# Rotary step of the second attention of layer two: neighbouring half blocks, cosine products in PSUM

## The reference, cut to what matters

```python
# hidden_states: (2, 512, 512); qkv_w: (512, 1536); H = 32 heads, D = 16
def _rope(x, cos, sin):
    x1, x2 = jnp.split(x, 2, axis=-1)
    return jnp.concatenate([x1 * cos - x2 * sin, x2 * cos + x1 * sin], axis=-1)
# q, k, v = (normalised x) @ qkv_w + qkv_b, 32 heads each; q, k = _rope(q), _rope(k)
# causal softmax(q k^T * scale) v, then out_w, out_b and the residual
```

## Time and profile before

| | |
|---|---|
| time, median of 3 runs | 2277.07 us (2275.81 to 2278.4) |
| profiled execution: its time, its span | 2275.74 us, 2273.9 us |
| mean granted TensorE clock | 0.953 |
| busy share of the span: PE, DVE, ACT, POOL | 92%, 62%, 51%, 36% |
| attn1b's first projection matmul starts | 1901.31 us |
| its first score matmul starts | 1999.34 us |

### The profile page before, as it was taken

The page is one execution under the profiler, slowest core; times in us unless marked ns, Lnnn a source line. Parts: engine busy times, 40 slices in busy tenths (PEclk is TensorE's granted clock), DMA queues, the critical chain, the costliest instruction groups (busy, mean ns, idle before and its releaser), DMA issues. The chain is left out here.

```text
span 2273.9 us, 33298 instructions
## 1 busy us (share of the span) xinstructions
PE 2086.4 (92%) x11568; PEld 1485.0 (65%) x11568; DVE 1400.9 (62%) x2517; ACT 1164.6 (51%) x2691; POOL 824.2 (36%) x996
## 2 busy tenths in 40 slices
PE   5999987999999999999987789999999887899988
PEld 3333345777888888888765667777777574654457
DVE  5788564536666666666646456666665565567756
ACT  4677543245656656656535455555555433235553
POOL 0000100235645645545520254555445213247611
PEclk9899978999999999999999799999999987989999
DMA  3000022671112112111011433443333003543301
GB/s 116 1 1 1 5 76 74 193 232 38 46 39 66 46 39 66 44 41 47 20 38 49 123 93 91 112 109 91 99 95 96 34 19 94 163 70 76 73 24 38
DMA packets 95427, 157.77 MB, mean 69 GB/s; under 512 B 11727, under 2 KB 33359, under 8 KB 93086
## 3 DMA queue, kind: packets, MB, share of 16 engines
q1 hardware_dynamic: 85662, 134.26, 20.6%
q0 software_dynamic: 9600, 21.38, 3.9%
HBM read 90.58 MB, written 31.46 MB: 54 GB/s over the span
## 5 line engine op out<-in xcount | busy, mean ns | idle before, releaser
L2528 POOL TENSOR_TENSOR attn1a_probs<-attn1a_probs,attn1a_recip 128x128 f32<-128x128 f32 (+3 forms) x256 | 178.9, 720 | 234.6 <-DVE attn1a_recip L2711 234.0
L1889 POOL TENSOR_TENSOR attn0b_probs<-attn0b_probs,attn0b_recip 128x128 f32<-128x128 f32 (+3 forms) x256 | 196.1, 787 | 184.9 <-DVE attn0b_recip L2133 184.9
L2584 ACT ACTIVATE attn1a_probs<-attn1a_scores,attn1a_negmax 128x128 f32<-128x128 f32 (+3 forms) x256 | 132.7, 523 | 175.4 <-DVE attn1a_negmax L2697 174.1
L1993 ACT ACTIVATE attn0b_probs<-attn0b_scores,attn0b_negmax 128x128 f32<-128x128 f32 (+3 forms) x256 | 132.7, 524 | 122.3 <-DVE attn0b_negmax L2126 121.7
L1440 DVE TENSOR_REDUCE attn0a_negmax<-attn0a_by_query 128x2 f32<-128x1024 f32 x128 | 151.9, 1219 | 11.8 <-PE attn0a_by_query L1557 11.8
L2697 DVE TENSOR_REDUCE attn1a_negmax<-attn1a_scores 128x2 f32<-128x256 f32 (+3 forms) x128 | 105.4, 823 | 71.4 <-PE attn1a_scores L2886 71.3
L1882 POOL TENSOR_TENSOR attn0b_q_cos<-attn0b_q_cos,attn0b_q_swap 128x512 f32<-128x512 f32 x64 | 84.3, 1317 | 159.9 <-DVE attn0b_q_swap L2115 159.9
L2001 ACT ACTIVATE attn0b_probsT_hi<-attn0b_turned 128x256 fp32r<-128x256 f32 (+3 forms) x128 | 90.1, 704 | 88.2 <-PE attn0b_turned L2277 86.6
L2126 DVE TENSOR_REDUCE attn0b_negmax<-attn0b_scores 128x2 f32<-128x256 f32 (+3 forms) x128 | 105.0, 820 | 46.7 <-PE attn0b_scores L2266 46.7
L2898 PE MATMUL attn1a_turned<-ident_f,attn1a_probs 128*128 128x128 f32 x640 | 116.1, 279 | 8.6 <-DVE attn1a_probsT L2705 7.3
L2112 DVE TENSOR_TENSOR attn0b_q_cos<-attn0b_aux,attn0b_cos_q 128x512 f32<-128x512 f32 x60 | 41.5, 691 | 116.2 <-ACT attn0b_q_swap L2014 116.2
(11 more groups left out here) (509 smaller groups left out, 6249.5 us busy)
## 6 DMA issues: line engine op xcount, KB each, us to landing
pre<-in_b_o SPq DMA_DIRECT2D x16, 1024.0 KB, 5.4
attn1a_qT<-attn1a_stage SPq DMA_DIRECT2D x128, 128.0 KB, 2.4
attn1a_qT<-attn1a_stage SPq DMA_DIRECT2D x64, 256.0 KB, 3.8
attn0b_vals<-attn0b_v_out SPq DMA_DIRECT2D x16, 512.0 KB, 3.9
attn0b_keys<-attn0b_part SPq DMA_DIRECT2D x32, 256.0 KB, 4.2
pre<-in_b_q SPq DMA_DIRECT2D x8, 1024.0 KB, 7.6
attn0b_kT<-attn0b_keys SPq DMA_DIRECT2D x64, 128.0 KB
pre<-in_b_kv SPq DMA_DIRECT2D x5, 1024.0 KB, 6.8
```

The lines of the kernel that those rows point to most:

```text
L1889: pool.tensor_tensor(x, x, recip[:, r % DEEP, e:e + 1].broadcast_to([P, (qt + 1) * P]), ALU.mult).then_inc(s_scaled, 1)
L1993: act.activation(probs[:, r % DEEP, e, 0:width], scores[r % 2][:, e, 0:width], ACT.Exp, bias=negmax[:, r % 2, e:e + 1], accum_out=sums[:, ...
L2528: pool.tensor_tensor(x, x, recip[:, r % DEEP, e:e + 1].broadcast_to([P, (qt + 1) * P]), ALU.mult).then_inc(s_scaled, 1)
L2584: act.activation(probs[:, r % DEEP, e, 0:width], scores[r % 2][:, e, 0:width], ACT.Exp, bias=negmax[:, r % 2, e:e + 1], accum_out=sums[:, ...
```

## The change

The columns of the key and query weights are reordered on the host so that a block holds one half (x1 or x2) of 16 heads, and its neighbour, the next block in the order, the other half of the same heads. The permutation matmul and its DMA go. ACT still writes raw (now four deep). DVE makes (projection + bias) x cosine straight from the projection's bank into one of four PSUM banks that the stage otherwise leaves idle (`turned`: by_key x 2, aux, out); POOL multiplies raw by the sines; DVE adds or subtracts the neighbour's sine product in the PSUM bank. PE now waits for the cosine product of block i - 2 instead of its raw. Splitting into hi and lo runs two blocks behind. The four pieces of a weight third are split one at a time (after blocks 1, 2, 4, 6 for the second third; 9, 10, 11, 12 for the last), and the last third's remainders are made by POOL. SP issues the last third's load behind the stores of part 6 instead of part 1, and the output weights' load behind everything, once the first attention tiles are in. A store now covers 16 heads x 8 rows instead of 8 heads x 16 rows.

```diff
-    blocks = [(kind, mt, b) for kind in range(KINDS) for mt in range(KT) for b in range(BATCH)]
+    RAWS = 4
+    SPLIT_SECOND, SPLIT_THIRD, SPLIT_THIRD_LO = (1, 2, 4, 6), (9, 10, 11, 12), (9, 11, 13, 14)
+    blocks = [(kind, 2 * half_heads + part, b) for kind in range(KINDS) for half_heads in range(2)
+              for b in range(BATCH) for part in range(2)]
...
-            raw, by_cos = take_sb("raw", [P, 2, SEQ]), take_sb("by_cos", [P, 2, SEQ])
-            turned_sb = take_sb("turned", [P, 2, SEQ])
...
+        turned = [by_key[0][:, :], by_key[1][:, :], aux_flat, out[:, :, :].rearrange("p t q -> p (t q)")]
+
+        def turned_block(k):
+            return k ^ 1
...
-            sp.dma_start(swap[:, :], d["c1_swap"]).then_inc(s_load, 16)
...
             def spread_out(i):
-                kind, mt, b = blocks[i]
-                into = spread_raw[kind][8 * mt:8 * mt + 8, :, bass.ts(b, SEQ)]
+                kind, mt, b = blocks[turned_block(i)]
+                heads, part = divmod(mt, 2)
+                into = spread_raw[kind][16 * heads:16 * heads + 16, :, bass.ts(b, SEQ)]
+                at = HD // 2 * part
                 sp.wait_ge(s_hi, i + 1)
-                sp.dma_start(into[:, 0:HD, :], part_hi[:, i % 2, :].bitcast(F32)).then_inc(s_spread[i % 2], 16)
+                sp.dma_start(into[:, at:at + HD // 2, :], part_hi[:, i % 2, :].bitcast(F32)).then_inc(s_spread[i % 2], 16)
                 sp.wait_ge(s_lo, i + 1)
-                sp.dma_start(into[:, HD:2 * HD, :], part_lo[:, i % 2, :].bitcast(F32)).then_inc(s_spread[i % 2], 16)
+                sp.dma_start(into[:, HD + at:HD + at + HD // 2, :], part_lo[:, i % 2, :].bitcast(F32)).then_inc(
+                    s_spread[i % 2], 16)
 
             load_weights(1)
             sp.dma_start(out_bias[:, :], d["c1_bo"].partition_broadcast(P)).then_inc(s_out_bias, 16)
             for i in range(NB):
                 spread_out(i)
-                if i == 1:
+                if i == SPLIT_SECOND[-1]:
                     load_weights(2)
-                if i == BLOCKS_OF_KIND + 1:
-                    sp.wait_ge(s_whi, 3 * KT)
-                    sp.wait_ge(s_wlo, 3 * KT)
-                    m.prefetch(sp, 0, w_in, d["c1_wo"].rearrange("(k p) o -> p k o", p=P))
+            for loaded in (s_kload[0], s_qload[0]):
+                sp.wait_ge(loaded, LOADED)
+            sp.wait_ge(s_whi, 3 * KT)
+            sp.wait_ge(s_wlo_v, KT)
+            m.prefetch(sp, 0, w_in, d["c1_wo"].rearrange("(k p) o -> p k o", p=P))
...
-            def times_cos(i):
-                kind, mt, b = blocks[i]
-                pool.wait_ge(s_raw, i + 1)
-                if i >= 2:
-                    pool.wait_ge(s_turned, i - 1)
-                pool.tensor_tensor(by_cos[:, i % 2, :], raw[:, i % 2, :], rope[:, kind, 0, :],
-                                   ALU.mult).then_inc(s_cos, 1)
+            def times_sin(k):
+                pool.wait_ge(s_raw, k + 1)
+                if k >= 2:
+                    pool.wait_ge(s_turned, k - 1)
+                pool.tensor_tensor(by_sin[:, k % 2, :], raw[:, k % RAWS, :], rope[:, blocks[k][0], 1, :],
+                                   ALU.mult).then_inc(s_sin, 1)
+
+            def split_value_weights(k):
+                pool.wait_ge(s_whi, KT * 2 + k + 1)
+                pool.tensor_tensor(w_lo[:, 0, k, :], w_in[:, k, :], w_hi[:, 0, k, :].bitcast(F32),
+                                   ALU.subtract).then_inc(s_wlo_v, 1)
...
-                times_cos(i)
+                times_sin(i)
+                if i in SPLIT_THIRD_LO:
+                    split_value_weights(SPLIT_THIRD_LO.index(i))
...
             def take(i):
                 kind, mt, b = blocks[i]
                 act.wait_ge(s_proj, i + 1)
-                if i >= 2:
-                    act.wait_ge(s_cos, i - 1)
-                    act.wait_ge(s_swap, i - 1)
-                act.activation(raw[:, i % 2, :], proj[i % 2], ACT.Identity,
+                if i >= RAWS:
+                    act.wait_ge(s_sin, i - RAWS + 1)
+                act.activation(raw[:, i % RAWS, :], proj[i % 2], ACT.Identity,
                                bias=bias_col[:, kind * KT + mt:kind * KT + mt + 1]).then_inc(s_raw, 1)
 
-            def split(i):
-                act.wait_ge(s_turned, i + 1)
-                if i >= 2:
-                    act.wait_ge(s_spread[i % 2], 16 * 2 * (i // 2))
-                act.activation(part_hi[:, i % 2, :], turned_sb[:, i % 2, :], ACT.Copy).then_inc(s_hi, 1)
+            def split(k):
+                act.wait_ge(s_turned, k + 1)
+                if k >= 2:
+                    act.wait_ge(s_spread[k % 2], 16 * 2 * (k // 2))
+                act.activation(part_hi[:, k % 2, :], turned[turned_block(k) % 4], ACT.Copy).then_inc(s_hi, 1)
...
+            for i in range(NB + 2):
                 if i < NB:
                     take(i)
-                if i == 1:
-                    split_weights(1)
-                if i >= 1:
-                    split(i - 1)
-                if i == BLOCKS_OF_KIND:
-                    split_weights(2)
+                if i >= 2:
+                    split(i - 2)
+                if i in SPLIT_SECOND:
+                    weights_hi(1, SPLIT_SECOND.index(i))
+                elif i in SPLIT_THIRD:
+                    weights_hi(2, SPLIT_THIRD.index(i))
...
-            def turn(i):
+            def weights_lo(third, k):
+                dve.wait_ge(s_whi, KT * third + k + 1)
+                dve.tensor_tensor(w_lo[:, third, k, :], w_in[:, k, :], w_hi[:, third, k, :].bitcast(F32),
+                                  ALU.subtract).then_inc(s_wlo, 1)
+
+            def times_cos(i):
                 kind, mt, b = blocks[i]
-                dve.wait_ge(s_swap, i + 1)
-                if i >= 2:
-                    dve.wait_ge(s_hi, i - 1)
-                dve.tensor_tensor(turned_sb[:, i % 2, :], by_key[i % 2][:, :], rope[:, kind, 1, :],
-                                  ALU.mult).then_inc(s_sin, 1)
-                dve.wait_ge(s_sin, i + 1)
+                dve.wait_ge(s_raw, i + 1)
+                if i >= 4:
+                    dve.wait_ge(s_lo, turned_block(i - 4) + 1)
+                dve.scalar_tensor_tensor(turned[i % 4], proj[i % 2], bias_col[:, kind * KT + mt:kind * KT + mt + 1],
+                                         rope[:, kind, 0, :], ALU.add, ALU.mult).then_inc(s_cos, 1)
+
+            def turn(k):
+                i = turned_block(k)
                 dve.wait_ge(s_cos, i + 1)
-                dve.tensor_tensor(turned_sb[:, i % 2, :], turned_sb[:, i % 2, :], by_cos[:, i % 2, :],
-                                  ALU.add).then_inc(s_turned, 1)
-
-            def split(i):
-                dve.wait_ge(s_hi, i + 1)
-                if i >= 2:
-                    dve.wait_ge(s_spread[i % 2], 16 * 2 * (i // 2))
-                dve.tensor_tensor(part_lo[:, i % 2, :], turned_sb[:, i % 2, :], part_hi[:, i % 2, :].bitcast(F32),
+                dve.wait_ge(s_sin, k + 1)
+                dve.tensor_tensor(turned[i % 4], turned[i % 4], by_sin[:, k % 2, :],
+                                  (ALU.subtract, ALU.add)[i % 2]).then_inc(s_turned, 1)
+
+            def split(k):
+                dve.wait_ge(s_hi, k + 1)
+                if k >= 2:
+                    dve.wait_ge(s_spread[k % 2], 16 * 2 * (k // 2))
+                dve.tensor_tensor(part_lo[:, k % 2, :], turned[turned_block(k) % 4], part_hi[:, k % 2, :].bitcast(F32),
                                   ALU.subtract).then_inc(s_lo, 1)
...
+            dve.wait_ge(s_load, 16)
+            for i in range(NB + 2):
+                if i < NB:
+                    times_cos(i)
+                    if i % 2 == 1:
+                        turn(i - 1)
+                        turn(i)
+                if i >= 2:
+                    split(i - 2)
+                if i in SPLIT_SECOND:
+                    weights_lo(1, SPLIT_SECOND.index(i))
...
-                    pe.wait_ge(s_raw, i - 1)
+                    pe.wait_ge(s_cos, i - 1)
...
-            def swap_halves(i):
-                pe.wait_ge(s_raw, i + 1)
-                if i >= 2:
-                    pe.wait_ge(s_sin, i - 1)
-                pe.matmul(by_key[i % 2][:, :], swap[:, :], raw[:, i % 2, :], start=True, stop=True).then_inc(s_swap, 1)
...
-                    pe.wait_ge(s_raw, NB - 1 + t)
+                    pe.wait_ge(s_cos, NB - 1 + t)
...
-                        pe.wait_ge(s_wlo, KT * 2 + k + 1)
+                        pe.wait_ge(s_wlo_v, k + 1)
...
-            for i in range(NB + 1):
-                if i < NB:
-                    project(i)
-                if i == 1:
-                    pe.wait_ge(s_load, 32)
-                if i >= 1:
-                    swap_halves(i - 1)
+            for i in range(NB):
+                project(i)
...
+    by_half = lambda x: t(x.reshape(-1, 2, 16, 2, 8), (0, 1, 3, 2, 4)).reshape(-1, DIM)
+    qkv = a["L1_attn_b_qkv_w"].reshape(DIM, 3, DIM)
```

(42 more changed lines are left out.)

14 lines of the change are left out of this document (6 added, 8 removed).

## The result

The changed kernel takes 2264.34 us (median of 6 runs, 2260.69 to 2269.03); the kernel before took 2277.74 us beside it (6 runs, 2275.81 to 2282.03). The ratio is 0.9941, with a 95% interval from 0.9927 to 0.9955: faster, by 13 us or so. The profiled execution took 2262.22 us.

A forecast was written before the change was run, and what follows sets the result against it. PE's own list was taken as the bound. The stage's terms summed to an end at 1987.1, 12.2 us earlier than 1999.3; from 2275.74 this made 2263.5, with 1.3 for the median 2264.8 us, range 2258.5 to 2272.5.

The forecast's parts named there:

- hole before block 12: PE waits for the last third of the weights, then its w_hi, raw and product: a hole of 2.6 us.
- wait before the values: Between block 15 and the value tiles: 0.7 us for the last product and POOL's last w_lo piece.
- hole before tile 2: Tile 0's value add queues on DVE behind the last three remainders: a 2.4 us hole, 1.5 for the clock behind it.
- Nothing gained up to block 4: Start of the stage: block 4 still starts near 1919.0; two saved swaps become idle time, 4.3 us in place of 1.84.
- Stores at 3.0 us: Part stores, DRAM side now led by 16 heads, not 8, land in 3.0 us instead of 5.05.
- Rival B: Stores still take 5.05 us to land: 6.5 us longer, 2271.3 us; chance 0.12.
- DVE writing PSUM: DVE's operations on PSUM take 0.68 us with a PSUM operand and 0.75 for the fused cosine product.
- rival C: DVE operations into PSUM take 1.05 us: the stage ends 5.7 us later, 2270.5 us; chance 0.08.
- rival A: Holes of 2.5 us do not bring PE's half clock: 3.5 us come back, 2261.3 us; chance 0.17.
- The third's load: SP's load of the last third of the weights, issued at 1938.1 behind part 6's stores, lands 5.9 us later.
- POOL's loads: Loads for the first attention steps: 18.6 us against 27.8 for the values, 9 us of cover; landing 3.4 us.
- Rivals D and E: D: more half-clock blocks on PE, 2277 us, chance 0.07. E: stores become the bound, 2285 us, slower, chance 0.06.

The follow-up runs named there:

- e3: The changed kernel with POOL's zeroing and copies spread over the gaps between its multiplications, its loads behind them: 2259.70 us, ratio 0.9934, stage 80.6 us.
- e1: The changed kernel with rows reordered so that each store's DRAM side is led by 8 again: 2271.89 us, ratio 0.9994, stage 91.9 us.
- e2: The kernel before, swaps kept, with rows reordered so that each store's DRAM side is led by 16: 2268.99 us, ratio 0.9977, stage 91.2 us.
- e4: The changed kernel with the second third split at blocks 1, 2, 3, 4, so the last third's load is issued earlier: 2261.88 us, ratio 0.9943.
- e7: The changed kernel with four spare matmuls (0.94 us) per block, putting the swaps' PE time back: 2268.37 us, ratio 0.9967, stage 90.5 us.
- e9: The changed kernel with the second third split earlier and spare matmuls before block 4's and value tile 2's waits: 2257.25 us, ratio 0.9919.

## Why the prediction was right, step by step

Terms of the stage, forecast and measured (from PE's timeline, whose main rows stand above; a block ends with its last matmul):

| term | forecast us | measured us |
|---|---|---|
| start to block 4 | 17.7 | 17.7 (hole 4.42, forecast 4.3) |
| block 4 at half clock | 4.9 | 4.6 |
| blocks 5 to 11 | 19.6 | 19.6 |
| hole before block 12 | 2.6 | 2.8 |
| blocks 12 to 15 | 13.2 | 13.0 |
| wait before the values | 0.7 | 0 |
| value tiles 0, 1 | 5.6 | 5.5 |
| hole before tile 2 | 2.4 | 2.9 |
| tiles 2 to 7 | 18.3 | 19.6 |
| last value add | 0.8 | 0.8 |
| stage | 85.8 | 86.5 |

- **Nothing gained up to block 4** held to a tenth: 17.7 us with the swaps or with none. The prediction speaks of two swaps saved there; the earlier trace rows show three before block 4, and three times 0.86 is what the hole grew by, 4.42 against 1.84. The cause was POOL, and e3 took it away.
- **Stores at 3.0 us** held (2.8 median, 2.93 for the one in the tail). The rule that the prediction cited (the Trainium skill, "DMA: Bandwidth & Descriptors", section "Why a DMA increments its semaphore by 16 and not by 1") agrees with the trace, in both directions by e1 and e2. Rival B's 6.5 us for stores of 5.05 us is what e1 tested; it measured 5.4, or 6.8 if the 1.4 us behind tile 2 are counted in.
- **DVE writing PSUM** costs 0.75 for the product and 0.70 for the turn, as taken; rival C is out.
- **No clock loss** (rival A) is out: the clock fell behind all three holes. The mis-sized term is here: 1.5 us behind tile 2, measured 3.0 from tile to tile. In e4, e7 and e9 it was 1.7, 1.7 and 0.1, so its size varies and the forecast was near the more common one. The 2.0 us for block 4 and for block 12 measured 1.6 each.
- **The third's load** landed in 6.4 us against 5.9 but was issued 0.6 us earlier in the stage (36.2 against 36.8). The hole was 0.2 us larger because block 11 ended 0.3 earlier. The 0.7 us before the values did not come: POOL's last w_lo piece was done by 1955.6, while PE went on at 1954.84 with tiles that need the earlier pieces first.
- **POOL's loads** were to have 9 us of cover. They began at 1966.23; the eight of the first steps were issued by 1970.4 and by the medians of their groups took 3.6 to 6.0 us to land, not 3.4: with 6.0, 7.4 us of cover. Rivals D and E (stores as the bound) did not come about; with landings at 2.8 us ACT waits for a store once, 3.5 us in the tail, where it waited 19.9 us before.
- The forecast of 2264.8 is closer to 2264.34 than its terms allow; that is luck. Of the 13.5 us between the two profiled executions, 1.3 more than forecast, 4.0 came ahead of the stage; against them stand 0.7 us less from the stage, 0.6 lost behind it and 1.4 more outside the span (3.2 against 1.8). What makes the start of the stage vary between executions stays open.

## What to carry to other kernels

Work taken off the busiest engine is worth only what the waits behind it let through: here 15.0 us of PE work cost 4.0, because the chains of POOL, of one late load and of one store in the tail each set a start time of their own. Look for the next chain at each place before the removal is counted, and move it in the same edit: three small moves gave 17.2 us of stage, more than the change's 11.5. For a store, look at how many rows lead its DRAM side: here, 256 KB led by 8 landed in 4.3 to 5.9 us (e1) at a DMA share near 0.5, led by 16 in 2.8.
